# The last group of the semilinear stage: where the gate's steps stand on VectorE, ScalarE and TensorE

## The reference

```python
x = x + cross_attention(layernorm(x), ctx)          # interpolated keys, 16 heads
x = x + semilinear(layernorm(x))                    # below
x = x + ffn(layernorm(x))                           # below

# semilinear: q, k, v by short convolutions, a recurrence over 2 chunks of 16 tokens
def step(carry, chunk):
    W_in, W_out = carry
    k_h = softmax(k W_in) * lr;  q_h = softmax(q W_in)
    o = q_h W_out + mask(q_h k_h^T) v
    W_out = W_out + k_h^T v
    for _ in range(2):                              # two gradient passes
        attn = softmax([W_in, W_out] [k, v]^T * scale)
        W_in, W_out = W_in + lr * ..., W_out + lr * ...
    return (W_in, W_out), o
# out = o @ Wo

# ffn: each token goes to the one of 8 experts with the largest gate score
scores = einsum('bsh,eh->bse', layernorm(x), gate_w)
chosen = argmax(scores, axis=-1)
out = x + expert_w[chosen] applied to layernorm(x)
```

## Time and profile before

| | us |
|---|---|
| median of 3 runs | 1219.58 |
| lowest, highest | 1213.76, 1223.68 |
| profiled execution | 1217.85 |
| its span, first to last instruction | 1216.1 |
| TensorE busy in the span | 1061.4 |
| VectorE busy | 813.3 |
| ScalarE busy | 494.7 |

### The profile page before, as it was taken

One profiled execution on the slowest core, in us unless ns is written; L12 is line 12 of the kernel. 1 busy time (PEld: TensorE's weight loads), 2 busy tenths in 40 slices (PEclk: granted clock), 3 DMA queues, 4 the chain that ended last, 5 costly groups with the idle time before them and its releaser, 6 DMA issues. The chain is left out here.

```text
span 1216.1 us, 18598 instructions
## 1 busy us (share of the span) xinstructions
PE 1061.4 (87%) x6220; PEld 787.6 (65%) x6220; DVE 813.3 (67%) x1592; ACT 494.7 (41%) x954; POOL 320.2 (26%) x265
## 2 busy tenths in 40 slices
PE   5993999999999963698999999999999987875997
PEld 4883566666666652477878776968696876763443
DVE  4565286778778883357888787979688876633332
ACT  1220255776676774134444443434252534310110
POOL 0344376677577662000000000000000000011553
PEclk9997898989889975788999999999899987765999
DMA  4281410222021000100010101010010031046541
GB/s 153 87 333 59 82 42 1 59 58 57 2 58 35 18 18 32 56 1 35 1 53 1 53 2 54 1 53 2 2 53 1 18 105 70 36 159 261 158 144 58
DMA packets 59924, 75.12 MB, mean 62 GB/s; under 512 B 37758, under 2 KB 42302, under 8 KB 57792
## 3 DMA queue, kind: packets, MB, share of 16 engines
q1 hardware_dynamic: 52384, 53.05, 13.7%
q0 software_dynamic: 5152, 12.59, 3.2%
q10 hardware_dynamic: 2304, 8.39, 1.7%
HBM read 56.71 MB, written 22.81 MB: 65 GB/s over the span
## 5 line engine op out<-in xcount | busy, mean ns | idle before, releaser
L1196 POOL COPY fw_x<-fw_x 128x1024 f32<-128x1024 f32 x8 | 8.3, 1040 | 536.0 <-DMA xh_scr<-fw_x 502.4
L556 POOL TENSOR_TENSOR aw_wtent<-aw_tent,aw_e 128x1760 f32<-128x1760 f32 x32 | 100.7, 3145 | 114.1 <-DVE aw_e L552 114.1
L745 PE MATMUL aw_psum_kv<-all_xWv,aw_c 128*128 128x512 f32 x256 | 124.6, 633 | 0.0
L528 POOL TENSOR_TENSOR aw_tent<-all_const,all_ix 128x1760 f32<-128x1760 f32 x32 | 100.6, 3145 | 5.1 <-POOL aw_wtent L556 4.6
L851 ACT ACTIVATE aw_cT<-aw_psum_av 32x256 f32<-32x256 f32 x128 | 80.5, 629 | 38.7 <-PE aw_psum_av L774 37.6
L733 PE MATMUL aw_psum_kv<-aw_c,all_xWk 128*128 128x352 f32 x256 | 81.6, 474 | 9.5 <-POOL aw_A L632 9.5
L2020 PE MATMUL ex_psum_y<-ex_We,ex_gT 128*128 x184 | 85.0, 607 | 0.0
L745 PEld LDWEIGHTS aw_psum_kv<-all_xWv,aw_c 128*128 128x128 f32 x256 | 49.4, 203 | 52.9 <-issue 51.1
L539 DVE TENSOR_TENSOR aw_prod<-aw_tent,aw_psum_s 128x1760 f32<-128x1760 f32 x32 | 63.5, 1984 | 23.8 <-ACT aw_tent L534 17.3
L1510 PE MATMUL fw_psum_front<-all_xWo,fw_cT 128*128 128x512 f32 x128 | 66.0, 666 | 11.7 <-DMA fw_cT<-c_scr 11.4
L733 PEld LDWEIGHTS aw_psum_kv<-aw_c,all_xWk 128*128 128x128 f32 x256 | 49.0, 196 | 35.2 <-POOL aw_A L632 9.6
(11 more groups left out here) (265 smaller groups left out, 2256.7 us busy)
## 6 DMA issues: line engine op xcount, KB each, us to landing
ex_We<-expert SPq DMA_DIRECT2D x1, 8192.0 KB, 22.4
aw_craw<-ctx SPq DMA_DIRECT2D x8, 704.0 KB, 4.8
xh_scr<-fw_x SPq DMA_DIRECT2D x10, 512.0 KB, 3.6
pj_x<-x_tok SPq DMA_DIRECT2D x8, 512.0 KB, 3.6
q_scr<-pj_QT ACTq DMA_DIRECT2D x8, 512.0 KB, 2.9
aw_Qb<-q_scr SPq DMA_DIRECT2D x32, 128.0 KB, 3.4
c_scr<-aw_cT ACTq DMA_DIRECT2D x8, 512.0 KB, 2.7
fw_cT<-c_scr SPq DMA_DIRECT2D x8, 512.0 KB, 4.8
```

The source lines that it names most:

```text
L528: return nc.gpsimd.tensor_tensor(self.tent[r][:], bc(rows, 1, self.nu * NK), bc(ix, 2, self.wr), ALU.subtract)
L556: return eng.tensor_tensor(self.wtent[:], self.tent[r][:], bc(self.e[:].rearrange("p u k -> p (u k)"), 2, self.wr), ALU.mult)
L745: mm = nc.tensor.matmul(ps_kv[:, j % 2, :], rows, Wv[:, c, :], start=(c == 0), stop=(c == KC - 1))
```

## The change

Only the last group and the end of the stage are touched; what is computed stays. On VectorE the first three `gate_stats` and `gate_rows` get other places. On ScalarE `gate_deviation` and `gate_copy` get earlier places, and `gate_deviation(3)` stands between `gate_copy(5)` and `gate_copy(6)`. On TensorE `gate_turn(0)` goes ahead of `si1`, and after the last projection the transposes run two groups ahead of the scores instead of one. On SP the stores of groups 4 to 6 go ahead of `store(LAST)`.

```diff
@@ SP, after the loop
-            for g in range(4):
+            for g in range(NG - 1):
                 gate_store(g)
             store(LAST)
-            for g in range(4, NG):
-                gate_store(g)
+            gate_store(NG - 1)
@@ VectorE, group
                 maxima(i, ch, 0)
-                if last:
-                    gate_stats(0)
                 if has_prev:
                     leave(t.prev(), i)
 ...
                 causal_products(i, 0)
+                if last:
+                    gate_stats(0)
                 normalise(t, ch, 0)
+                if last:
+                    gate_rows(0)
+                    gate_stats(1)
                 ahead("q2", "q1", "v1", "k2")
                 step_weights(i, ch, 0)
-                if last:
-                    gate_rows(0)
 ...
                 maxima(i, ch, 1)
                 if last:
-                    gate_stats(1)
+                    gate_rows(1)
 ...
                 normalise(t, ch, 1)
+                if last:
+                    gate_stats(2)
 ...
                 step_weights(i, ch, 1)
-                if last:
-                    gate_rows(1)
                 ahead("v3", "v2")
                 exponents(i, ch, 1)
                 weights(t, ch, 1)
+                if last:
+                    gate_rows(2)
@@ VectorE, after the loop
-            gate_stats(2)
             causal_products(NG, 1)
-            gate_rows(2)
@@ TensorE, group
                 blocks(i, back, "go0", KC, [(kt[:, g, :], atT[:, 1, g, :]) for g in by_g])
+                if last:
+                    gate_turn(0)
 ...
                 blocks(i, back, "so1", KC, [(wout[:, g, :], v[:, g, halves[0]]) for g in by_g])
                 if last:
-                    gate_turn(0)
                     gate_score(0)
                     gate_turn(1)
@@ TensorE, after the loop
             gate_score(4)
-            for g in range(5, NG):
-                gate_turn(g)
-                gate_score(g)
+            gate_turn(5)
+            gate_turn(6)
+            gate_score(5)
+            gate_turn(7)
+            gate_score(6)
+            gate_score(7)
@@ ScalarE, group
                 row_exponentials(i, 0)
+                if last:
+                    gate_deviation(0)
                 ahead("q2", "q1")
                 take(i, "ti0", atT[:, 0])
                 ahead("v1")
                 take(i, "to0", atT[:, 1])
                 if last:
-                    gate_deviation(0)
+                    gate_deviation(1)
+                    gate_copy(0)
 ...
-                if last:
-                    gate_copy(0)
                 row_exponentials(i, 1)
 ...
+                take(i, "vt1", vt[1][:])
                 if last:
-                    gate_deviation(1)
-                take(i, "vt1", vt[1][:])
+                    gate_deviation(2)
                 ahead("v3", "v2")
                 take(i, "wo", wrow[:])
-                exponentials(i, 1)
                 if last:
                     gate_copy(2)
+                exponentials(i, 1)
@@ ScalarE, after the loop
             gate_copy(3)
-            gate_deviation(2)
             take(NG, "o1", oT[:, :, P:2 * P])
-            for g in range(4, NG - 1):
-                gate_copy(g)
+            gate_copy(4)
+            gate_copy(5)
             gate_deviation(3)
+            gate_copy(6)
             gate_copy(NG - 1)
```

## The result

The changed kernel takes 1211.69 us in the median (1208.46 to 1216.39, 20 runs) against 1218.79 (1213.76 to 1223.68, 20 runs) for the kernel before. The ratio is 0.9957, with a 95% interval of 0.9944 to 0.9970: some 5.2 us faster. I had forecast 1221 and no change to tell, so the sign is wrong, and the time lies 1.3 us under the range.

A forecast was written before the change was run, and what follows sets the result against it. No engine fills the stretch; hand-over waits between VectorE, TensorE and ScalarE bound it. Terms +2.8, +1.0, -0.7, +1.45, +0.1, -1.9, -1.1 sum to +1.65 us, giving 1221 us, no change to tell; range 1213 to 1229.

The forecast's parts named there:

- The tail: TensorE behind the last projection: turning two groups ahead hides copy waits, 2.2 us less 1.1 left before the last score: -1.1 us.
- the case of fast scores: In the tail, if scores took 1.95 us, gate_turn(7) would wait about 0.7 us because of gate_deviation(3)'s table load.
- a rival, at 1215 us: Clock stays high in the tail: three scores fall from 3.58 to 1.95 us, two turns by 0.8 each; chance 0.10.
- +2.8: gate_stats(0) on VectorE, moved behind the causal products where nothing is waited for, delays normalise(0) in full: +2.8 us.
- +1.0: gate_rows(0) and gate_stats(1) between normalise(0) and step_weights(0): 4.85 us of VectorE work in a 3.89 us wait, +1.0 us.
- +1.45: gate_stats(2) between normalise(1) and step_weights(1): 4.2 us of VectorE work in a 2.75 us wait, +1.45 us, bounds 0.5 to 2.3.
- The table load: ScalarE before the second pass's exponentials: earlier gate copies let the exp table load finish before the maxima, -0.7 us.
- turned_softmax: TensorE: earlier copies let gate_score(2) and gate_turn(3) finish sooner, so turned_softmax starts when the weights are ready: -1.9 us.
- The exponential of the second chunk: ScalarE: gate_copy(2) and a table load ahead of exponentials(1) delay it by +0.1 us, bounds 0 and 0.8.
- width: The forecast's own spread: four more blocks at either clock level are 3.2 us, so 1218 to 1224 us.

The follow-up runs named there:

- tail_only: The kernel before with only the new order behind the last projection; ratio 0.9958 against the kernel before, 5.1 us faster.
- tail_fill: The kernel before, in its old order, with one dense matmul of unused result in each of the tail's three copy waits; ratio 0.9954, 5.6 us faster than before.
- stats0_back: The changed kernel with gate_stats(0) alone back at its old place ahead of leave(prev); ratio 0.9955 against the kernel before, 5.5 us faster.
- fit: The changed kernel with its VectorE steps put in waits meant to be long enough, and an early exp table load; ratio 0.9925 against before, 9.1 us faster.
- body_only: The changed kernel with the old order behind the last projection; ratio 0.9975 against the kernel before, 3 us faster.
- body_look: A second profile of body_only, unchanged; 59.41 us from the first maxima to the projection, tail 16.78 us.
- body_fill: body_only with tail_fill's dense matmuls of unused result in the tail's three copy waits; ratio 0.9971 against the kernel before, 3.5 us faster.
- fit_fill2: fit with dense matmuls of unused result in several TensorE waits, eleven ahead of the 32 matmuls that place the rows; ratio 0.9870 against before, 15.8 us faster.

## Why the prediction was wrong

**The tail is the step that failed.** The prediction counted -1.1 us there, the copy waits that the new order hides, and priced the scores at 3.58 us on either side. It measured -5.4 us. The waits came out nearly as I had them: 1.18 us ahead of the last score, where I had 1.1, and 0.80 of gate_turn(7) for VectorE, which I had at 0.7 for the case of fast scores. With both, TensorE idles 1.98 us in that tail, against 2.18 before. What was left out of the sum is the clock, 1.6 to 1.7 us for each of two scores and 0.8 to 0.9 for each of two transposes, 5.0 us together. It was there as a rival, at 1215 us and with a chance of 0.10, and two of its three scores came true. The measured 1211.69 lies 3.3 us below it; 0.8 of that is the kernel before, whose median of 20 runs is 1218.79 and not 1219.58, and the rest stays open.

**The evidence against that rival did not bear on it.** I held that from 1072 to 1076 TensorE was busy all the time at a clock of 0.50, so such small matmuls would not have the high clock. But that row shows work that found the clock low and did not raise it. (It also isn't all of eight columns, as I wrote: only the scores are, the transposes put out 128.) Whether the same work keeps the clock once it is high is another question, and the kernel after answers it: 5.00 busy of 5.00 us from 1068 to 1073, scores and transposes alone, at 1.00. The rule that I weighed and set aside, from the Trainium skill ("TensorE: Matmul & The Clock Gate", Why this matters for your kernels), was the better guide: without longer gaps between its matmuls, TensorE keeps the full clock. The traces of tail_only and tail_fill agree with it, with scores of 1.95 us where the gaps are closed. They do not agree on what a longer gap is: the ones that the section warns of are longer than the 0.80 us behind which the first of the three scores before was already slow, and there the measurement decides.

**The three VectorE terms held.** +2.8, +1.0 and +1.45 were forecast, +2.7, +0.8 and +1.4 measured. The third is the steadiest: in the four profiles with all the moves ahead of the projection the second step_weights comes 3.97 or 3.98 us behind ti1, where the four without them have 2.54. stats0_back takes the first away again in the trace, and fit the first two; for the third TensorE is waited for again in fit, but gi1 and go1 ran partly at the low level there (2.07 and 1.54 us against 1.14 and 1.06), and the station is still 3.81 us. The table load (-0.7 forecast, -0.8 measured) and turned_softmax (-1.9 and -1.9) held too.

**One ScalarE term was undersized.** The exponential of the second chunk came 0.9 us later, not 0.1: gate_turn(2) ran partly at the low clock (1.68 us against 1.04), and so did the four transposes ahead of it (1.06 against 0.64), so the copies ended at 1043.74 and the load followed. That is just beyond the bound of 0.8.

**Two terms were missing, both clock.** si1 and so1 took 1.16 and 1.06 us instead of 1.88 and 1.92, which gave 1.5 back, and in the stretch from turned_softmax to the projection, 0.8 longer, the causal scores took 2.09 us against 1.17 and gate_score(3) 3.58 against 2.26, while gate_turn(4) took 1.09 against 1.95. TensorE before, so1 and these two:

```profile
1021.28 1.92 PE L1487 MATMUL fw_psum_back<-fw_vT,fw_wout 128*128 128x128 f32 x8
...
1051.33 1.17 PE L1557 MATMUL fw_psum_back<-fw_qhT,fw_khT 32*128 32x128 f32 x32 [0.78 <-ACTq L240]
1052.50 2.26 PE L1598 MATMUL fw_psum_front<-fw_Wg,fw_hT 128*128 128x8 f32 x16
```

The first came in every one of the profiles with gate_turn(0) in the wait ahead of si1 (4.31 or 4.32 us to the second maxima, 5.84 in both of the kernel before); but tail_only and tail_fill, without that move, had 4.72 and 4.71, so the move is not shown to be the only cause. I had both as width, 3.2 us either way.

**The range was too narrow** because it was laid around a tail at the low clock, with the high one as a case of 0.10. Ahead of the projection the forecast's terms make +2.75 us; less the 1.5 us of clock that is +1.25, and the profiles with the moves show +0.3 (body_only, body_look), +1.4 (body_fill) and +2.4 (the changed kernel) against before's 59.1. That the sum fits here is in part luck, since tail_only and tail_fill, which have before's steps in that stretch, lie 4.1 below and 0.4 above it. I also held 1% for the least that a measurement can tell; the 95% interval of the ratio reaches 0.13% to either side, and the 0.43% were told.

## What to carry to other kernels

When short steps end a stage, price them at both levels of TensorE's clock, and ask what closes or opens its idle time; an order that hides a wait of 0.7 us can be worth several times that wait. A row that shows work at a low clock says nothing of what the same work would do on a high one, so give such a rival a chance that reflects not knowing. And before moving a step into a wait, hold its length against that wait: here 2.8 us stood in front of a step that waited for nothing, and fit, with the same steps in other waits, is the better kernel, by 4 us and with intervals that just touch.

## What the runs showed of the hardware

- Scores of 16 matmuls with 8 columns and transposes, behind a dense projection, went on at 1.00 while TensorE had no idle time (5.00 busy of 5.00 us from 1068 to 1073 in the changed kernel), but did not bring the level up again: before, the last three scores and the transposes between them all took the time of the low level, with 0.69 us of idle time ahead of the second and the third score. Dense matmuls of 128x512 did: in fit_fill2 TensorE stood at 0.50 from 1079.4 to 1081 and at 0.96 in the mean from 1081 to 1091, and the 32 matmuls behind them ran at 1.00.
- Behind idle times of 0.80 to 1.18 us the high level was lost, though not each time: the changed kernel kept it over 0.80 us ahead of gate_turn(7), stats0_back lost it over 0.81 us at the same place. Longer ones did not always lose it either: over 2.79 us ahead of ti1 the changed kernel kept it (1.09 us), stats0_back did not (1.96 us). So the length of one idle time does not decide it; what else does is not shown here.
- A table load on ScalarE cost 1.28 us, and its activation followed 1.29 us after the load began (1043.76 to 1045.05).
